# Output projection of an attention block as three products of rounded high and low parts

## The reference

```python
x = x + 0.5 * ffn(layernorm(x))
x = x + attention(layernorm(x))        # 16 heads of 64, rotary embedding, causal softmax
x = x + 0.5 * ffn(layernorm(x))

# attention
q, k, v = x @ wq.T, x @ wk.T, x @ wv.T            # split into 16 heads, q and k rotated
probs = softmax(where(causal, q @ k.T / 8, -inf))
out = probs @ v                                   # heads joined again: 1024 features
return out @ wo.T                                 # 1024 -> 128: the output projection
```

## Time and profile before

| | |
|---|---|
| median of 3 runs | 1323.15 us (1322.53 to 1323.75) |
| the profiled execution | 1324.65 us, of it 1322.9 us from the first to the last instruction (the span) |
| TensorE matmuls busy | 1247.7 us, 94% of the span |
| ACT busy | 914.8 us, 69% |
| DVE busy | 754.2 us, 57% |
| POOL busy | 444.5 us, 34% |
| mean granted clock of TensorE | 0.983 of full speed |

### The profile page before, as it was taken

One profiled execution on the slowest core, in us unless ns is written; L12 is line 12 of the kernel. 1 busy time (PEld: TensorE's weight loads), 2 busy tenths in 40 slices (PEclk: granted clock), 3 DMA queues, 4 the chain that ended last, 5 costly groups with the idle time before them and its releaser, 6 DMA issues. The chain is left out here.

```text
span 1322.9 us, 26897 instructions
## 1 busy us (share of the span) xinstructions
PE 1247.7 (94%) x7456; PEld 869.4 (66%) x7456; DVE 754.2 (57%) x1787; ACT 914.8 (69%) x1946; POOL 444.5 (34%) x288
## 2 busy tenths in 40 slices
PE   5986699999999999999999999999999999999898
PEld 2543566777777677767676767676767676766465
DVE  5574446665556666565656565656565656554354
ACT  3654467777777777777777777777777777777574
POOL 5132443333333333333333333333333333330000
PEclk8997799999999999999999999999999999999999
DMA  7122444454544445454545454545454544431000
GB/s 275 45 95 88 124 104 130 110 134 107 142 106 129 121 110 140 97 146 104 145 105 145 105 145 105 145 105 145 105 144 104 135 107 130 108 84 36 1 29 36
DMA packets 107198, 147.80 MB, mean 112 GB/s; under 512 B 11808, under 2 KB 61344, under 8 KB 107040
## 3 DMA queue, kind: packets, MB, share of 16 engines
q1 hardware_dynamic: 106768, 146.65, 41.8%
q10 hardware_dynamic: 400, 0.79, 0.3%
HBM read 36.24 MB, written 10.49 MB: 35 GB/s over the span
## 5 line engine op out<-in xcount | busy, mean ns | idle before, releaser
L936 DVE CUSTOM_DVE_ANT_0 probs<-wide,tri_mask 128x1024 f32<-128x1024 f32 (+7 forms) x512 | 386.0, 756 | 431.3 <-PE wide L637 424.8
L821 ACT ACTIVATE probs<-probs,neg_max 128x1024 f32<-128x1024 f32 (+7 forms) x512 | 395.6, 774 | 160.8 <-DVE neg_max L936 156.8
L832 ACT ACTIVATE shared_a<-bank 128x512 f32<-128x512 f32 (+2 forms) x640 | 339.6, 548 | 111.6 <-PE bank L653 107.8
L653 PE MATMUL bank<-ident,probs 128*128 128x128 f32 x2304 | 366.0, 278 | 3.5 <-ACT shared_a L832 1.3
L653 PEld LDWEIGHTS bank<-ident,probs 128*128 128x128 f32 x2304 | 266.2, 141 | 153.3 <-issue 108.6
L636 PE MATMUL wide<-k_hh,q_hl 128*128 128x512 f32 (+3 forms) x768 | 292.6, 383 | 5.9 <-DMA k_hh<-parts 2.2
L670 PE MATMUL bank<-shared_a,v_cur 128*64 128x256 f32 (+3 forms) x1792 | 297.2, 453 | 0.0
L637 PE MATMUL wide<-k_low,q_hl 128*128 128x512 f32 (+3 forms) x768 | 257.9, 343 | 0.0
L92 POOL TENSOR_TENSOR rotated<-terms,cross 128x1024 f32<-128x1024 f32 x62 | 147.7, 2383 | 291.0 <-DVE cross L86 282.8
L670 PEld LDWEIGHTS bank<-shared_a,v_cur 128*64 128x64 f32 x1792 | 108.7, 136 | 113.2 <-issue 88.2
L1049 POOL COPY inv_wide<-inv 128x512 f32<-128x512 f32 x64 | 39.1, 611 | 376.0 <-DVE inv L944 343.4
(11 more groups left out here) (114 smaller groups left out, 1323.6 us busy)
## 6 DMA issues: line engine op xcount, KB each, us to landing
q_hl<-parts SPq DMA_DIRECT2D x254, 128.0 KB, 2.8
k_hh<-parts SPq DMA_DIRECT2D x254, 128.0 KB, 2.7
v_cur<-shared_b SPq DMA_DIRECT2D x32, 512.0 KB, 5.8
k_low<-parts SPq DMA_DIRECT2D x63, 256.0 KB, 4.2
xn_cur<-xn_scratch SPq DMA_DIRECT2D x15, 1024.0 KB, 5.8
w_qk<-w_scratch SPq DMA_DIRECT2D x32, 256.0 KB, 3.1
w_scratch<-first_w_parts SPq DMA_DIRECT2D x8, 512.0 KB, 3.1
xn_scratch<-shared_a SPq DMA_DIRECT2D x8, 512.0 KB, 3.1
```

Source lines behind the costliest of these rows:

```text
L653: last = nc.tensor.transpose(ring[at % 2][:, col:col + P], probs[g][:, h, OFFSET[g][r] + j * P:OFFSET[g][r] + (j + 1) * P], ident[:])
L821: nc.scalar.activation(own, own, ACT.Exp, bias=neg_max[g][:, col], scale=-1.0, accum_out=sums[g][:, col]).then_inc(probs_done, 1)
L832: nc.scalar.activation(turned[:, slot, to], ring[at % 2][:, 0:w * len(heads)], ACT.Copy).then_inc(ring_free[at % 2], signals)
L936: nc.vector.tensor_tensor_reduce(out=part_of_probs(g, k), in0=wide_banks[k % 2][:, x0:x1], in1=tri_mask[:, SEQ - (x1 - x0):], scale=1.0, s ...
```

## The change

The projection of `head_out` by wo is made of three f32r matmuls in place of one float32 matmul (which has two records in the trace). For that, ACT rounds `head_out` into a high part (`round_head`), DVE subtracts it from `head_out` for the low part (`low_head`), and the projection waits for both (`head_split`). `normalise` waits until the low part before was made. wo is loaded whole at the start (`wo_plain`, 512 KB), split by POOL in two instructions at the end of the first half block, stored to DRAM (1 MB), and each pair's part (128 KB in place of 64) is loaded from there.

```diff
 # first half block, POOL
                     for_each(pool, PAIRS_OF_CHUNKS - 1, body)
+                    pool.wait_ge(ahead.wo_arrived, 16)
+                    nc.gpsimd.tensor_copy(wo_parts[:, :, 0, :], ahead.wo_plain[:]).then_inc(wo_high_done, 1)
+                    pool.wait_ge(wo_high_done, 1)
+                    nc.gpsimd.tensor_tensor(wo_parts[:, :, 1, :], ahead.wo_plain[:], wo_parts[:, :, 0, :].bitcast(F32),
+                                            ALU.subtract).then_inc(wo_low_done, 1)
                     pool.wait_ge(o.high_done, 1)
                     low_half(nc, o, 0)
 # first half block, SP
                 if norm_b:
+                    sp.wait_ge(wo_low_done, 1)
+                    sp.dma_start(ahead.wo_out, wo_parts[:].bitcast(F32)).then_inc(ahead.wo_stored, 16)
                     sp.wait_ge(o.low_done, 1)
                     for h in range(2):
                         fill_qk(sp, o, 0, 0, h)
 # attention, TensorE
                 if g == 0:
                     pe.wait_ge(wo_loaded[u], 16 * (i + 1))
-                pe.wait_ge(head_done, 2 * p + g + 1)
+                pe.wait_ge(head_split, 2 * p + g + 1)
                 may_write(of, at)
-                nc.tensor.matmul(ring[at % 2][:], wo_cur[:, u, :], head_out[:], start=True, stop=True).then_inc(ring_full, 1)
+                out = ring[at % 2][:]
+                nc.tensor.matmul(out, wo_cur[:, u, 0, :], head_parts[:, 0, :], start=True, stop=False)
+                nc.tensor.matmul(out, wo_cur[:, u, 0, :], head_parts[:, 1, :], start=False, stop=False)
+                nc.tensor.matmul(out, wo_cur[:, u, 1, :], head_parts[:, 0, :], start=False, stop=True).then_inc(ring_full, 1)
 # attention, ACT
+            def round_head(p, g, before):
+                act.wait_ge(head_done, 2 * p + g + 1)
+                if some(before):
+                    act.wait_ge(ring_full, before)
+                nc.scalar.activation(head_parts[:, 0, :], head_out[:], ACT.Copy).then_inc(head_high_done, 1)
...
                 keep_turned(p, u, 0, 4)
                 exponential(p, 1, 2)
+                if has_prev:
+                    round_head(p - 1, 1, ring_count(p - 1, RING_OUT[0]))
                 keep_turned(p, u, 0, 5, 1 if has_prev else 2)
                 exponential(p, 1, 3)
...
                 keep_turned(p, u, 1, 4)
                 keep_turned(p, u, 1, 5)
+                round_head(p, 0, ring_count(p, RING_OUT[1]))
                 next_exponential(2)
                 next_exponential(3)
...
+            round_head(ALL_PAIRS - 1, 1, ring_count(ALL_PAIRS - 1, RING_OUT[0]))
 # attention, DVE
                 dve.wait_ge(out_step, NK * p + KEYS[0] + KEYS[1] * g)
+                if some(2 * p + g):
+                    dve.wait_ge(head_split, 2 * p + g)
                 nc.vector.tensor_tensor(head_out[:], out_bank[:], inv_sum[:], ALU.mult).then_inc(head_done, 1)
+
+            def low_head(p, g):
+                dve.wait_ge(head_high_done, 2 * p + g + 1)
+                nc.vector.tensor_tensor(head_parts[:, 1, :], head_out[:], head_parts[:, 0, :].bitcast(F32),
+                                        ALU.subtract).then_inc(head_split, 1)
...
                 max_of(p, 1, 2)
                 max_of(p, 1, 3)
+                if has_prev:
+                    low_head(p - 1, 1)
                 ahead(1)
                 max_of(p, 1, 4)
                 max_of(p, 1, 5)
...
                 next_max(3)
+                low_head(p, 0)
                 next_max(4)
                 next_max(5)
                 add_to_x(i // (PAIRS // 2), 0, RING_OUT[0], p)
...
             normalise(ALL_PAIRS - 1, 1)
+            low_head(ALL_PAIRS - 1, 1)
             add_to_x(BATCH - 1, 1, 0, ALL_PAIRS)
 # attention, SP
             def load_wo(u, w_index):
-                sp.dma_start(wo_cur[:, u, :], wo_pairs[w_index]).then_inc(wo_loaded[u], 16)
+                sp.dma_start(wo_cur[:, u, :, :].bitcast(F32), wo_split[:, w_index]).then_inc(wo_loaded[u], 16)
...
+            sp.wait_ge(ahead_of.wo_stored, 16)
             load_wo(0, 0)
 # start of the kernel, SP
                     sp.dma_start(sin[:], sin_d).then_inc(tables_arrived, 16)
+                    sp.dma_start(wo_plain[:], wo_pairs).then_inc(wo_arrived, 16)
```

More of the change, by code:

```diff
@@ L30 @@
 EXP_AND_LN = "natural_log_exp_and_others"
-Ahead = namedtuple("Ahead", "w_plain w_arrived w_out w_qk w_v xn_cur qk_loaded v_loaded xn_loaded")
+Ahead = namedtuple("Ahead", "w_plain w_arrived w_out w_qk w_v xn_cur qk_loaded v_loaded xn_loaded wo_plain wo_arrived wo_out wo_stored")
 Operands = namedtuple("Operands", "parts terms cross rotated k_hh q_hl k_low proj_full proj_free sum_done high_done low_done "
@@ L167, in macaron_half @@
             w_high_done, w_low_done, w_stored = sem("w_high_done"), sem("w_low_done"), sem("w_stored")
+            wo_parts = sb("wo_parts", [P, PAIRS, 2, DIM], F32R)
+            wo_high_done, wo_low_done = sem("wo_high_done"), sem("wo_low_done")
             xn_b_high_done, xn_b_low_done = sem("xn_b_high_done"), sem("xn_b_low_done")
@@ L507, in _, with attention @@
                         sp.wait_ge(stored[u], 16 * PAIRS_OF_CHUNKS)
-def attention(nc, x, xn_dram, xn_stored, wo_pairs, ahead_of, o, constants,
+def attention(nc, x, xn_dram, xn_stored, wo_split, ahead_of, o, constants,
               turned_mem, v_stage, wide_banks, banks):
@@ L521, in sem @@
             return ctx.enter_context(nc.semaphore(name))
-        wo_cur = sb("wo_cur", [P, 2, DIM])
+        wo_cur = sb("wo_cur", [P, 2, 2, DIM], F32R)
+        head_parts = sb("head_parts", [P, 2, CHUNK], F32R)
+        head_high_done, head_split = sem("head_high_done"), sem("head_split")
         o.k_hh.append([sb(f"k_hh1{h}", [P, SEQ], F32R) for h in range(2)])
@@ L1157, in macaron @@
     xn_dram = nc.dram_tensor("xn_scratch", [P, 2, TOKENS], F32, kind="Internal").ap()
+    wo_split = nc.dram_tensor("wo_scratch", [P, PAIRS, 2, DIM], F32, kind="Internal").ap()
     w_split = nc.dram_tensor("w_scratch", [PAIRS, P, 2, 512], F32, kind="Internal").ap()
@@ L1191, in macaron @@
         w_plain = first_half.enter_context(nc.sbuf_tensor("w_plain", [P, PAIRS, 512], F32))
-        ahead = Ahead(w_plain, w_arrived, w_split, w_qk, w_v, xn_cur, qk_loaded, v_loaded, xn_loaded)
+        wo_plain = first_half.enter_context(nc.sbuf_tensor("wo_plain", [P, PAIRS, DIM], F32))
+        wo_arrived, wo_stored = sem("wo_arrived"), sem("wo_stored")
+        ahead = Ahead(w_plain, w_arrived, w_split, w_qk, w_v, xn_cur, qk_loaded, v_loaded, xn_loaded, wo_plain, wo_arrived,
+                      wo_split, wo_stored)
         xn_stored, x_stored = ([sem(f"{n}_stored{u}") for u in range(2)] for n in ("xn", "x"))
@@ L1253, in macaron @@
         first_half.close()
-        attention(nc, x, xn_dram, xn_stored, wo_pairs, ahead, o,
+        attention(nc, x, xn_dram, xn_stored, wo_split, ahead, o,
                   (tri_mask, ident), shared_a, v_stage, wide_banks, banks[4:8])
@@ L1284 @@
         "w_qkv": np.ascontiguousarray(np.concatenate([wqk, wv], axis=2).transpose(1, 0, 2)),
-        "wo_pairs": np.ascontiguousarray(np.asarray(L0_attn_wo).T.reshape(PAIRS, P, DIM)),
+        "wo_pairs": np.ascontiguousarray(np.asarray(L0_attn_wo).T.reshape(PAIRS, P, DIM).transpose(1, 0, 2)),
         "cos_d": np.ascontiguousarray(np.concatenate([c * to_q, c * to_q, c, c])),
```

## The result

The changed kernel takes 1356.05 us (median, 1354.87 to 1357.42) against 1322.84 us for the kernel before: a ratio of 1.0253 (95% interval 1.0235 to 1.0271), 33 us slower. The forecast was 1361. The profiled execution took 1356.08 us; its span is 1354.4 us.

A forecast was written before the change was run, and what follows sets the result against it. TensorE was taken to set the pace, with its saving swallowed by waits on ACT and DVE. Terms 30.7 + 0.8 + 1.5 + 3.5 + 1.1 = 37.6 us on a median of 1323.15 gave 1361 us, forecast 1352 to 1375, range 1344 to 1375.

The forecast's parts named there:

- First place: Group 1: subtraction ahead of max(1,4) makes ACT's copy late; TensorE stalls at turn(0,7), 1.06 us in 29 pairs, 30.7 us.
- hand-overs of nothing: Lower bound at group 1: rounding at 0.53 us and no hand-over time give 0.85 us a pair, -6 us.
- Last two pairs: Group 1 without a rope unit, so max(1,4) has more room: 0.39 us each, 0.8 us.
- Second place: Group 0: saving swallowed, turn(9) late but old wait covers nearly all: 0.1 us in 15 pairs, 1.5 us.
- The lock: Group 0: DVE's subtraction is held up by POOL's rope addition, from 630.15 to 632.36.
- the cover: Group 0: TensorE's old 0.74 us wait for the addition to x hides the delay, leaving 0 to 0.18 us.
- Start: POOL's split of the output weights ahead of low_half(0) delays it without cover: 3.5 us.
- End: Last projection waits for rounding, subtraction and two hand-overs, less the cheaper matmuls and last group 0: 1.1 us.
- Sum: 30.7 + 0.8 + 1.5 + 3.5 + 1.1 = 37.6 us added, giving 1361 us at the median.
- the margin of 0.43 us: Rival at turn(0,7): copy late by less than margin minus saving, TensorE never stands: 1318 us, chance 0.05.
- given back at the sums' transposes: Rival: TensorE stands at turn(0,7) but less at turn_sums, 0.4 us a pair left: 1342 us, chance 0.08.
- the dearer place: Rival at group 0: POOL's cast gets in first, subtraction ends 1.1 us later: 26 us more, 1387, chance 0.07.

The follow-up runs named there:

- experiment 1: Changed kernel with group 1's subtraction low_head(p-1,1) moved behind max(1,4), ahead of max(1,5): 1325.22 us, ratio 1.0003 to the kernel before.
- experiment 5: Changed kernel with the subtraction low_head(p-1,1) between the rope unit and max(1,4): 1337.05 us, ratio 1.0091 to the kernel before.
- experiment 3: Changed kernel with the projection again one float32 matmul of head_out and the weights' high part, all else kept: 1355.04 us, ratio 1.0230 to the kernel before.
- Experiment 2: Changed kernel with group 0's subtraction low_head(p,0) moved behind next_max(4): 1356.40 us, ratio 1.0237 to the kernel before.
- experiment 7: Kernel before, only reordered: group 0 projected ahead of score(5) and added to x ahead of max(5): 1315.46 us, ratio 0.9929.
- experiment 8: Changed kernel with both subtractions moved back, POOL's weight split early, and group 0 projected ahead of score(5), added ahead of max(5): 1308.74 us, ratio 0.9882.
- experiment 10: experiment 8 with the very last projection as two float32 matmuls of head_out, without rounding or subtraction: 1305.96 us, ratio 0.9865 to the kernel before.
- experiment 4: Changed kernel without the split of head_out, three f32r matmuls kept, start kept, output not the reference's: 1321.07 us, ratio 0.9981 to the kernel before.
- experiment 9: experiment 1 plus POOL's early weight split and the very last projection as two float32 matmuls without rounding or subtraction: 1320.03 us, ratio 0.9972.

## Why the prediction was right

- **First place: the mechanism held, the size was off.** The stall is 0.87 us a pair in place of 1.06, so 25.35 us over 29 pairs, not 30.7. The forecast took 0.10 us from ACT to DVE where the trace has 0.04 (626.92 to 626.96), and 0.14 from ACT's copy to TensorE where it has 0.06 (630.79 to 630.85); the rounding took 0.61 us, not 0.63, and the copy 0.57, not 0.60. So max(1,4) is 1.48 us late, not 1.57, and the four differences make up the 0.19. This term makes 5.35 of the 6.2 us by which the sum of 37.6 lay above the profiles' 31.4. The forecast's lower bound of 0.85 us for "hand-overs of nothing" took off only the hand-over from ACT to DVE; without both it is 0.72. Experiments 1 and 5 show that the chain through max(1,4) is the cause, experiment 3 that the saving is swallowed behind it.
- **Last two pairs:** they cost 0.25 us in all, against 0.8.
- **Second place:** it cost 0.00 us against 0.1 in 15 pairs. The lock was as forecast (2.25 us, worked out as 2.21); the cover was whole, not nearly whole. Experiment 2 shows that removing the delay only gives back the older wait.
- **Start:** the split itself delays low_half(0) by 3.4 us, against 3.5. That the ledger shows 3.00 in pair 0 is in part luck: the changed kernel's profile lost 1.6 us more to the clock ahead of the first product of v, and the kernel before lost 1.5 to it in pair 0 (both below).
- **End:** it cost 1.2 us at the last addition to x, against 1.1. What the forecast left out is the clock of the second half block, 1.6 us in this run.
- **Sum:** 3.0 + 25.35 + 0.25 + 1.2 + 1.6 = 31.4; the two spans, rounded, differ by 1354.4 less 1322.9, 31.5. The medians differ by 33.2, since the profiled execution of the kernel before, at 1324.65 us, lay above the median; 37.6 is 4.4 above 33.2.
- **Rivals:** the margin of 0.43 us was overrun by the copy, so the saving did not arrive; nothing of the stall was given back at the sums' transposes, since the ledger keeps its 0.87 there; the lock was not the dearer place. All three fell.

## What to carry to other kernels

An instruction that waits costs its queue, not itself: before adding one, ask which instruction behind it feeds the bottleneck, and put it where the engine would stand anyway; here one move on DVE was worth 31 us. A cheaper instruction on the bottleneck is worth nothing ahead of a wait (experiment 3); first move the wait (experiment 7), then the saving arrives (experiment 8). When one wait is removed, look for the wait it had covered before counting a gain (experiment 2).

## What the runs showed of the hardware

```profile
96.00:100.00 4.00, 3.94 (x9) 2.34 (x10) 2.24 (x6) 0.00 (x0) 0.00 (x0) 0.63 0.35 131
```

```profile
96.00:100.00 4.00, 3.90 (x14) 2.53 (x15) 2.67 (x7) 0.81 (x2) 0.00 (x0) 1.00 0.35 131
...
179.00:184.00 5.00, 5.00 (x25) 4.32 (x24) 2.29 (x5) 2.32 (x4) 3.22 (x2) 0.66 0.02 6
```

So the changed kernel lost 1.6 us at 96 us: from that matmul to the next one of its line that waits it takes 14.18 us (96.06 to 110.24), the kernel before 12.56. The edit doesn't decide it. In the twelve profiles the same wait stands there, 1.92 to 1.93 us, and the clock from 96 to 100 us is below 0.70 in five (the changed kernel and experiments 3, 5, 7 and 10) and 1.00 in seven; experiment 7 (0.57) has the instructions of the kernel before up to there, experiments 1, 2 and 4 (1.00) those of the changed kernel. The kernel before lost 1.5 us in pair 0, behind a wait of 1.86 us for a DMA at 178.81 us; there the changed kernel waited 1.65 us and kept 1.00 in the 5 us that follow (from that matmul to the second sums' transposes it took 14.70 us, the kernel before 16.22). With the wait that is 0.2 us shorter, that is why the ledger begins at 4.72 and then shows 3.00. With the start of the changed kernel, the first product of v begins at 143.2 to 143.7 us in experiments 1, 2 and 4, 3.2 to 3.6 after the kernel before's 140.08, and at 144.7 and 145.4 us in 3 and 5, where the clock fell; in the changed kernel it is at 145.1.

At the end the fall is regular. In all seven kernels that split head_out there, TensorE stands 2.23 to 2.24 us ahead of the last projection and 1.06 us behind it, and the second half block starts at the lower clock (0.58 from 1274 to 1278 us in the changed kernel, 1.00 from 1244 to 1248 us before); the changed kernel's rows:

```profile
1272.05 0.50 PE L701 MATMUL bank<-head_parts,wo_cur 128*128 128x512 f32 x1 [2.23 <-DVE head_parts L979]
...
1274.07 1.46 PE L193 MATMUL bank<-x,mean_of 128*128 128x512 f32 x2 [1.06 <-PEq L525]
1276.32 2.08 PE L193 MATMUL bank<-x,mean_of 128*128 128x512 f32 x2 [0.78 <-DVE shared_b L375]
```

The three that stand 0.86 us there (the kernel before, experiments 4 and 7) have 1.10 us in the place of 1.46. From that matmul to the end the seven take 80.3 to 82.1 us, the three 77.2 to 78.7: some 3 us on top of the 1.2 that the split costs by its own instructions. Starting at the upper level does not always keep it: the kernel before is at 0.57 from 1252 to 1256 us and experiment 7 at 0.68 from 1244 to 1248, while experiment 4 stays at 1.00 from 1240 to 1260. Experiments 9 and 10, at 80.7 and 79.2 us, don't settle how much of it a shorter wait brings back.
